# First layer's running states kept as 32x32 blocks of four heads, built by 32-column products and applied on the diagonal tiles of TensorE

## The reference, cut to what matters

```
def _L0_attn_ref(x, W1, b1, W2, b2):
    kqv = x @ W1 + b1
    k, q, v = jnp.split(kqv, 3, axis=-1)
    k, q, v = (to_heads(k), to_heads(q), to_heads(v))      # (8, 16, 512, 8)
    mask = jnp.tril(jnp.ones((t, t), dtype=bool))
    attn = jnp.where(mask, jnp.einsum('bhqd,bhkd->bhqk', q, k), 0.0)
    out = jnp.einsum('bhqk,bhkd->bhqd', attn, v)
    return out.transpose(0, 2, 1, 3).reshape(bs, t, d) @ W2 + b2

x = x + _L0_attn_ref(_layernorm(x, axis=-1), ...)
x = x + _L0_ffn_ref(_layernorm(x, axis=-1), ...)
```

## Time and profile before

| | |
|---|---|
| median of 3 runs | 1473.63 us (1473.41 to 1477.93) |
| span of the profiled execution | 1432.3 us |
| the profiled execution's own time | not recorded apart from its span; the median is 41.3 us above that span |
| granted TensorE clock, mean | 0.886 |
| busy in the span | PE 1099.4, PEld 814.9, DVE 834.6, ACT 544.6, POOL 484.7 us |
| first layer's attention stage | 8 us to 206 us of the span |

### The profile page before, as it was taken

One profiled execution on the slowest core, in us unless ns is written; L12 is line 12 of the kernel. 1 busy time (PEld: TensorE's weight loads), 2 busy tenths in 40 slices (PEclk: granted clock), 3 DMA queues, 4 the chain that ended last, 5 costly groups with the idle time before them and its releaser, 6 DMA issues.

```text
span 1432.3 us, 39482 instructions
## 1 busy us (share of the span) xinstructions
PE 1099.4 (77%) x16860; PEld 814.9 (57%) x16860; DVE 834.6 (58%) x2486; ACT 544.6 (38%) x919; POOL 484.7 (34%) x555
## 2 busy tenths in 40 slices
PE   5899938992766398376788888889888887762996
PEld 3677727992655266253455565656565564442885
DVE  6577744654877311525857768585858675733343
ACT  3223102221542132141456373737465553450442
POOL 3123331332767300424131324324231403022576
PEclk9999969996987599577899999999999999776998
DMA  9940033653200241211112021222121100103685
GB/s 375 397 180 18 19 112 105 198 160 114 89 15 23 62 95 47 66 51 52 50 45 61 12 69 52 56 58 63 51 62 48 46 22 11 53 20 102 150 212 112
DMA packets 89204, 126.46 MB, mean 88 GB/s; under 512 B 14914, under 2 KB 67396, under 8 KB 88612
## 3 DMA queue, kind: packets, MB, share of 16 engines
q1 hardware_dynamic: 72868, 107.79, 24.0%
q0 software_dynamic: 11936, 14.04, 4.4%
q10 hardware_dynamic: 4224, 2.10, 0.5%
HBM read 53.10 MB, written 44.83 MB: 68 GB/s over the span
## 4 chain that ended last, share of the span: by engine, by line
PE 26%; DVE 19%; ACT 8%; DMA 3%; POOL 3%; issue 3%; SPq 2%; POOLq 0%; DVEq 0%; ACTq 0%
DVE mx L1497 9%; ACT MW L1710 4%; PE ps L791 2%; PE ps L713 2%; PE ps L965 2%; PE ps L699 2%; PE ps L805 2%; DVE mx L1488 2%; PE ps L908 2%; PE ps L899 2%; PE ps L821 1%; PE ps L900 1%; DMA MW<-l_moe_dram 1%; DVE X L1028 1%; DVE bst L1000 1%
## 5 line engine op out<-in xcount | busy, mean ns | idle before, releaser
L1497 DVE TENSOR_REDUCE mx<-ps 128x2 f32<-128x1024 f32 (+3 forms) x176 | 188.5, 1120 | 33.2 <-PE ps L938 33.1
L1710 ACT ACTIVATE MW<-ps 128x1024 f32<-128x1024 f32 x160 | 154.6, 1028 | 74.9 <-PE ps L950 74.4
L1830 POOL DMA_INDIRECT xs<-xr,sidu x96 | 95.4, 994 | 141.9 <-DVE sidu L1158 104.2
L1773 POOL TENSOR_SCALAR rst<-bmv 128x4 f32<-128x4 f32 x64 | 15.6, 243 | 246.2 <-DVE bmv L1003 241.1
L713 PE MATMUL ps<-tmpA,MW 128*128 128x256 f32 x336 | 92.7, 392 | 6.9 <-DMA MW<-l_moe_dram 3.5
L965 PE MATMUL ps<-MW,Vp 128*16 128x128 f32 x2560 | 87.8, 279 | 3.6 <-ACT MW L1710 3.5
L531 PE MATMUL ps<-W,xr 128*128 128x128 f32 x192 | 38.3, 335 | 64.5 <-DVE xr L1013 35.3
L1858 POOL DMA_INDIRECT out_dram<-qf,toku x46 | 71.5, 1554 | 42.7 <-DVE toku L1320 34.5
L699 PE MATMUL ps<-MW 128*128 128x128 f32 x672 | 82.0, 275 | 3.0 <-DVE qf L1305 1.5
L699 PEld LDWEIGHTS ps<-MW 128*128 128x128 f32 x672 | 78.5, 192 | 3.4 <-issue 3.3
L938 PE MATMUL ps<-K,Q 64*128 64x512 bf16 (+3 forms) x512 | 62.8, 319 | 22.2 <-DVE mx L1497 15.3
(11 more groups left out here) (319 smaller groups left out, 2537.9 us busy)
## 6 DMA issues: line engine op xcount, KB each, us to landing
xs<-hb SPq DMA_DIRECT2D x66, 384.0 KB, 4.2
MW<-l_moe_dram SPq DMA_DIRECT2D x19, 768.0 KB, 5.5
MW<-l_moe_dram SPq DMA_DIRECT2D x23, 578.0 KB, 5.1
Q<-spl SPq DMA_DIRECT2D x48, 128.0 KB
K<-spl SPq DMA_DIRECT2D x48, 128.0 KB
Q<-spm SPq DMA_DIRECT2D x48, 128.0 KB
K<-spm SPq DMA_DIRECT2D x48, 128.0 KB
tmpA<-xs SPq DMA_DIRECT2D x42, 132.0 KB, 2.2
```

The costliest lines, as they stand in the source:

```text
L1497: V.tensor_reduce(out=mx[1][:, :, s0:s0 + ns, t], in_=p.rearrange("p (e n) -> p e n", e=2)[:, :, 0:ns * nk].rearrange("p e (s k) -> p e s ...
L1710: A.activation(P3[k % 2][:, 1024 * half:1024 * half + 1024], p, ACT.Exp).then_inc(drained[u], 1)
L1830: G.indirect_dma_start(out=xs[L], out_offset=bass.IndirectOffsetOnAxis(ap=sidu[:, 4 * b + t:4 * b + t + 1], axis=0), in_=src[:, t, 0:128 i ...
```

## The change

The states are kept as four 32x32 blocks (the heads of one group of four against each other) instead of one 128x128 matrix. A token tile is multiplied once for each group and added to all later states at the same time, since the moving operand repeats the same 32 columns of v by a stride of 0: 192, 128 and 64 columns for tiles 0, 1 and 2. The first half of each tile is then added to the state in its middle by 32-column products. That makes 12 products with 128 rows and 16 with 64 rows, each with 32 columns of weights, on the four column tiles. DVE masks 128x224 instead of 128x896. In `l0_o` each of the 7 states is applied by four 32x32 products on the diagonal tiles, all 28 of them ahead of the products of L659, and within one PSUM bank after the other.

```diff
-        l0_S = [kflat[i][:, 512:1408].rearrange("p (c d) -> p c d", c=7) for i in range(2)]
+        l0_S = [kflat[i][:, 512:736].rearrange("p (c d) -> p c d", c=7) for i in range(2)]
...
-        def v_dense(i, t, lo, hi):
-
-            v = vpad[i][lo:hi, t, :, :, :]
-            return bass.AP(tensor=v.tensor, offset=v.offset, ap=[list(v.ap[0]), [128, 4], [40, 4], [1, 8]])
+        def v_group(i, t, g, rows, copies):
+
+            v = vpad[i][0:rows, t, g, :, :]
+            return bass.AP(tensor=v.tensor, offset=v.offset, ap=[list(v.ap[0]), [0, copies], [40, 4], [1, 8]])
...
-                    for c in range(1, 8):
-                        t, half = divmod(c, 2)
-                        o = p[:, 128 * (c - 1):128 * c]
-                        for tt in range(t):
-                            m = PE.matmul(o, ktok[i][:, tt, :], v_dense(i, tt, 0, 128), start=(tt == 0), stop=(tt == t - 1 and not half))
-                        if half:
-                            m = PE.matmul(o, ktok[i][0:64, t, :], v_dense(i, t, 0, 64), start=(t == 0), stop=True)
+                    for t in range(4):
+                        if t < 3:
+                            for g in range(4):
+                                PE.matmul(p[32 * g:32 * g + 32, 32 * (2 * t + 1):224], ktok[i][:, t, 32 * g:32 * g + 32],
+                                          v_group(i, t, g, 128, 6 - 2 * t), start=(t == 0), stop=(t == 2),
+                                          tile_position=(0, 32 * g), skip_group_check=True)
+                        for g in range(4):
+                            m = PE.matmul(p[32 * g:32 * g + 32, 64 * t:64 * t + 32], ktok[i][0:64, t, 32 * g:32 * g + 32],
+                                          v_group(i, t, g, 64, 1), start=False, stop=True,
+                                          tile_position=(0, 32 * g), skip_group_check=True)
...
+                    for c in (1, 0):
+                        for t in range(4):
+                            for g in range(4):
+                                if 2 * t + c:
+                                    PE.matmul(p[32 * g:32 * g + 32, 512 * c + 64 * t:512 * c + 64 * t + 64],
+                                              l0_S[i][32 * g:32 * g + 32, 2 * t + c - 1, :],
+                                              qf[i][32 * g:32 * g + 32, 128 * t + 64 * c:128 * t + 64 * c + 64],
+                                              start=(t == 1 - c), stop=False, tile_position=(32 * g, 32 * g), skip_group_check=True)
                     for t in range(4):
-                        for c in range(2):
-                            if 2 * t + c:
-                                PE.matmul(p[:, 512 * c + 64 * t:512 * c + 64 * t + 64], l0_S[i][:, 2 * t + c - 1, :],
-                                          qf[i][:, 128 * t + 64 * c:128 * t + 64 * c + 64], start=True, stop=False, skip_group_check=True)
...
-                                                  l0_P(i, t // 2, g // 2)[64 * c:64 * c + 64, o:o + 64], start=(2 * t + c == 0 and j == 0), stop=(j == 3),
+                                                  l0_P(i, t // 2, g // 2)[64 * c:64 * c + 64, o:o + 64], start=False, stop=(j == 3),
...
-                    V.tensor_tensor(out=l0_S[i].rearrange("p c (h e) -> p c h e", h=H),
-                                    in0=p[:, 0:896].rearrange("p (c h e) -> p c h e", c=7, h=H),
-                                    in1=w("hmask_nat").unsqueeze(1).unsqueeze(3).broadcast_to([128, 7, H, 8]), op=ALU.mult).then_inc(drained[u], 1)
+                    V.tensor_tensor(out=l0_S[i].rearrange("p c (h e) -> p c h e", h=4),
+                                    in0=p[:, 0:224].rearrange("p (c h e) -> p c h e", c=7, h=4),
+                                    in1=w("jmask").unsqueeze(1).unsqueeze(3).broadcast_to([128, 7, 4, 8]), op=ALU.mult).then_inc(drained[u], 1)
```

## The result

Slower. After: 1481.85 us, median of 5 runs (1476.91 to 1486.20); before, beside it: 1473.41 us (5 runs, 1469.42 to 1477.93). The ratio is 1.007 with a 95% interval of 1.0039 to 1.0100, 8 to 10 us more, where 24 us less was predicted.

A forecast was written before the change was run, and what follows sets the result against it. TensorE was taken to set the stage's pace, VectorE not far behind. The period falls from 19.7 to 16.7 us, 21 us over 7 periods, plus 3.3 in the last batch: 24.3 saved, 1449.3 us, range 1440 to 1466.

The forecast's parts named there:

- the products: TensorE's l0_st falls from 4.93 to 2.2 us, l0_o from 5.4 without its gap to 3.8.
- VectorE's mask: The mask falls from 1.09 to about 0.4 us, in itself worth nothing.
- The new wait for ScalarE's drain of `l0_q`: Behind l0_st, TensorE waits 0.9 us in each period until ScalarE frees the PSUM unit.
- The issue gap: In l0_o's dense run, a second gap in a third of periods: 0.3 us average, ends 0 and 1.5.
- rival C: Fetching instructions: two gaps each period, 1.5 us more in three loaded ones, 0.6 in others; 1455 us, chance 0.15.
- The two stretches at the low clock stay: In the changed stage, TensorE's low-clock stretches stay as many as before.
- rival B: TensorE's clock falls every period, six more times, costing 19 us: 1468 us; chance 0.12 for four or more.
- rival A: l0_o's diagonal tiles, writing one PSUM bank, take turns: 1485 us, or 1465 at 0.05 a record; chance 0.10.
- The 41.3 us laid around the span: Time added around the forecast span of 1408.0 us, taken from the median, giving 1449.3 us.
- The dear end of the output step: Upper end for l0_o: 9.0 us if the diagonal products run one after the other.
- the 5.0 us in the range: Dear end of l0_o used for the range's upper end, beside 3.2 us for l0_st.

The follow-up runs named there:

- x_warm: The changed kernel plus one whole product of 512 columns behind each l0_st, into an unused bank; ratio to before 1.0003.
- x_diag: The kernel before with its old l0_st, VectorE cutting out the diagonal blocks, and the change's diagonal l0_o; ratio to before 1.0088.
- x_pad28: The kernel before plus 28 products of one column ahead of l0_o; 1483.27 us against 1470.78.
- x_half: The changed kernel with 112 of the 256 own-chunk records of a batch left out; no measured time or ratio is given.
- before again: The kernel before, unchanged, profiled once more beside the experiments; span 1472.6 us.
- x_wide_warm: x_wide plus one whole product of 512 columns behind each l0_st; ratio to before 1.0064.
- x_wide: The changed kernel's l0_st, with VectorE spreading its blocks over 128x128 states and l0_o as before the change; ratio to before 1.0023.

## Why the prediction was wrong

**Right: the products.** Against the forecast, at full clock (`x_warm`'s period): `l0_st` 138.56 to 140.28, 1.7 us where 2.2 was forecast (in after itself 1.8 to 4.3, with short gaps in four of the eight); the diagonal products 0.92 us for 1.0; `l0_o` 145.87 to 151.45 less its gap, 3.9 us for 3.8. VectorE's mask (L1278, 224 columns) took 0.36 us for 0.4. The new wait for ScalarE's drain of `l0_q` came where it was expected in six of the eight batches, with 0.4 to 1.4 us where 0.9 was forecast. TensorE's work in a period is 15.65 us at full clock with the added product in it, so some 14.7 without, against 19.4 before.

**Wrong: the step "The issue gap".** It put 0.3 us on a period and 1.5 at its far end, as a second gap in a third of the periods. The price is that of a rate. In after, 128 records of L666 with their 128 weight loads take 1.47 us at full clock, but the next block of as many started no sooner than 3.45 us after the last (108.88 to 112.33), and while the zeroing DMAs fill the queues (DMA share 1.03) 4.83 us after it:

```profile
39.83 2.04 PE L666 MATMUL ps<-MW,Vp 64*32 64x64 f32 x128 [4.21 <-issue]
44.66 0.65 PE L666 MATMUL ps<-MW,Vp 64*32 64x64 f32 x23 [2.79 <-issue]
```

Before, four runs of whole products with their changes of shape lay between the narrow ones and stretched the use. The change took these slow pieces out and put 56 fast records in their place: what it saved of array time in `l0_o`, it mostly waited for instructions instead. In the whole stage the issue idle grew by 21.8 us, 2.7 a batch. That is beyond rival C too, which had two gaps a period, but of a total of 0.6 to 1.5 us more, and beyond the end of 1.5. The Trainium skill (Runtime: NRT & Kernel Launch, Instruction fetch mechanics) says that instructions are refilled in blocks of 256 and that crossing from one to the next is mostly hidden. The block agrees with the distance of 128 records and 128 weight loads between the gaps above; that it is hidden does not hold in this kernel, where 13 such gaps cost 27.0 us.

**Wrong: the step "The two stretches at the low clock stay", and the chance of rival B.** B had the mechanism, and its sign in the profile, a clock under 0.9 between 90 and 160 us, is there in each period. But it got 0.12, on the ground that a gap of 0.40 us had left the clock full. The gaps after are longer, and there is a second place at which the clock fell. It fell behind gaps of about 2 us in the dense run: `x_diag`, with the old `l0_st`, has 0.88 between 96 and 163 us, and `x_pad28`, whose gaps there are under 0.9 us, has 1.00. And it fell behind the narrow `l0_st` with its wait: `x_half` has half the gaps and stays at 0.82, and `x_warm` has all the gaps and one large product in the wait, and gets back to 0.89 and 10 us.

**How the two add up**, in the three middle periods: TensorE's work saves 4.7 us a period at full clock (19.4 to 14.7). The low clock takes 4.6 of it back (19.3 us busy instead of 14.7), and the idle time adds 2.6 (3.1 instead of 0.5). Sum +2.5, as measured (22.4 against 19.9). By this sum the low clock alone would have left the time of before, and the idle time alone a gain of 2.1 us a period; together they are a loss. The two aren't independent, since part of the falls stand behind the gaps. The prediction gave each a chance for itself and never added them.

**Refuted: rival A.** 56 diagonal records in 0.91 us are 16 ns each, not 50 or 100, on four row tiles and in one PSUM bank at a time, each tile on its own partitions. The rule of the Trainium skill (TensorEngine Tiling, Gotcha 1, PSUM Pressure), that different row tiles cannot access one bank at once, is not borne out by the time of these products. Nor are the 25 ns that the Trainium skill (TensorE: Matmul & The Clock Gate, section on 56 against 53.3 ns) has as the least from start to start: 128 records of L666 took 1.47 us, under 12 ns each.

**Wrong too: the base.** The 41.3 us laid around the span weren't there. The profiled execution of after took 1476.91 us for a span of 1475.1, so only 1.8 us lie around it. The profile of before was of an execution some 39 us faster than the median, and faster almost wholly behind the stage of the change (its stage ended 3.2 us earlier than that of before again). It lies at the level of the two groups near 1436 us. The profiles show one thing that goes with the level: from 240 to 1430 us, TensorE's issue idle is 15.8 to 19.9 us in each profile of the groups near 1471 us and 0.3 to 3.6 in the others. This doesn't touch the sign.

**Small slips in the prediction's own working.** The dear end of the output step is given as 9.0 us, but 0.4, 2.4 and the 5.6 of rival A make 8.4, and the 5.0 us in the range has no working. In the earlier trace rows a clock of 0.57 over 8.0 us is work for 4.6 us and not 4.9, so a fall costs 3.4 us. Neither changes the outcome.

**Open.** Why the block takes 3.45 us to arrive was not measured by itself; that it takes 4.83 us while the DMA share is 1.03 points at the transfers they share. What exactly lowers the clock isn't separated either: the rows show two places at which it fell, but narrow tiles and idle time came together at both. The short gaps inside `l0_st` and what `x_wide_warm` pays for its product stay open too.

## What to carry to other kernels

TensorE's time in a stage of many tiny products is not the sum of the products: ask how many instructions lie in the densest stretch and how fast they arrive, and treat slow products between fast ones as the time in which the next block comes. A step that makes products smaller and leaves waits can lose its gain to the granted clock, so price both together, and look for the version that does the same with fewer and larger products first. Take a profile's own time, not the median of other runs, as what lies around its span.

## What the runs showed of the hardware that was not expected

- A block of 128 products and 128 weight loads was followed by the next no sooner than 3.45 us later (after, `x_diag`, `x_pad28`), and 4.55 to 5.10 us later under full DMA queues (`x_warm`, after); a dense run uses it up in 1.5.
- 32x32 tiles on the diagonal ran side by side within one PSUM bank, 16 ns a record (56 in 0.91 us).
- A useless whole product of 512 columns, 0.96 us in each of 8 batches, made the changed kernel 10 us faster (ratio 1.0070 to 1.0003), by the granted clock (0.81 to 0.89 in the window from 27 to 190 us). With `x_wide`, whose `l0_st` mostly leaves no wait, it gained nothing (1.0023, and 1.0064 with the product).
- The kernel before took 1471 and 1472 us in two groups of runs, 1437 and 1435 in two others. TensorE's issue idle behind the stage goes with it: 18.4 us in before again, 3.6 in the profile of the earlier trace rows.
